# Condition weights read as four consecutive rows per partition, in a fused adaLN and feed-forward kernel on Trainium2

## The reference

```python
out = jnp.einsum('bsd,bdh->bsh', x, W[cat_ids]) + b[cat_ids][:, None, :]   # condition stage
x = act_qdq(out)
up = act_qdq(x @ lpbq_dequant(w_up).T)
gate = act_qdq(x @ lpbq_dequant(w_gate).T)
gate = act_qdq(gate * fixed_qdq_u16(jax.nn.sigmoid(gate)))
return x_in + act_qdq(gate * up) @ lpbq_dequant(w_down).T
```

## Time and profile before

| | |
|---|---|
| median of 3 runs | 970.74 us (969.74 to 971.73) |
| the profiled execution's own time | 973.98 us |
| its span, first to last instruction | 972.1 us |
| TensorE busy | 891.0 us, 92% of the span |
| VectorE busy | 656.1 us, 67% |
| ScalarE busy | 422.9 us, 43% |
| share of the chain that ended last | PE 87%, DMA 7%, ACT 3%, DVE 1% |

### The profile page before, as it was taken

How to read it: one execution, slowest core, us unless ns; L and a number is a source line. 1 busy time by engine, 2 the same in 40 slices (tenths; PEclk the granted TensorE clock), 3 DMA queues, 4 the chain that set the end, 5 groups by cost and what they waited for, 6 DMA issues and landing times.

```text
span 972.1 us, 13026 instructions
## 1 busy us (share of the span) xinstructions
PE 891.0 (92%) x4712; PEld 478.5 (49%) x4712; DVE 656.1 (67%) x771; ACT 422.9 (43%) x448; POOL 3.0 (0%) x12
## 2 busy tenths in 40 slices
PE   6999999999999999999999999970059999999998
PEld 6998995444444444444444444430024444444443
DVE  1355869655757454379899889559977777775511
ACT  1112326223223323299798872229865444444000
POOL 0000000000000000000000000000000000000000
PEclk9999999999999999999999999995569999999999
DMA  8998982544474343779999735999986799988221
GB/s 294 380 386 283 325 314 86 155 154 159 151 248 129 119 142 136 220 287 421 409 371 394 255 143 216 415 422 358 417 318 260 292 339 340 342 307 303 86 87 65
DMA packets 93875, 255.89 MB, mean 263 GB/s; under 512 B 32082, under 2 KB 32082, under 8 KB 93842
## 3 DMA queue, kind: packets, MB, share of 16 engines
q1 hardware_dynamic: 58354, 198.72, 55.3%
q10 hardware_dynamic: 35488, 56.77, 16.6%
HBM read 175.51 MB, written 73.66 MB: 256 GB/s over the span
## 4 chain that ended last, share of the span: by engine, by line
PE 87%; DMA 7%; ACT 3%; DVE 1%; issue 1%; SPq 0%; ACTq 0%; POOL 0%; DVEq 0%
PE bank L737 16%; PE bank L739 16%; PE bank L738 16%; PE bank L684 11%; PE bank L772 7%; PE bank L773 6%; PE bank L774 6%; DMA up_ring<-up_scratch 3%; DMA x_ring<-in_x_dram 2%; ACT umag L633 2%; PE bank L669 1%; PE wt_bank L772 1%; PE bias_bank L772 1%; PE wt_bank L773 1%; PE wt_bank L774 1%; PE bias_bank L773 1%
## 5 line engine op out<-in xcount | busy, mean ns | idle before, releaser
L548 ACT ACTIVATE stage<-bank 128x512 f32<-128x512 f32 x192 | 112.0, 594 | 224.6 <-PE bank L739 170.3
L772 PE MATMUL bank<-wt_down,o_even 128*128 128x512 f16 x192 | 74.0, 385 | 65.9 <-DVE o_even L1205 65.9
L996 DVE TENSOR_REDUCE tile_max<-stage 128x1 f32<-128x1536 f32 (+1 forms) x62 | 108.4, 1749 | 33.8 <-ACT stage L548 30.7
L737 PE MATMUL bank<-xq_head,wt_up 128*128 x336 | 127.4, 379 | 0.9 <-ACT stage L548 0.9
L737 PE MATMUL bank<-xq_head,wt_gate 128*128 (+1 forms) x336 | 127.4, 379 | 0.3 <-DVE xq_head L983 0.3
L738 PE MATMUL bank<-xq_head,wt_up 128*128 x336 | 127.3, 379 | 0.0
L739 PE MATMUL bank<-xq_head,wt_up 128*128 x336 | 127.3, 379 | 0.0
L739 PE MATMUL bank<-xq_head,wt_gate 128*128 (+1 forms) x336 | 127.3, 379 | 0.0
L738 PE MATMUL bank<-xq_head,wt_gate 128*128 (+1 forms) x336 | 127.3, 379 | 0.0
L684 PE MATMUL bank<-xt,w_ring 128*128 128x128 f32 x1024 | 123.4, 280 | 2.2 <-ACT xt L486 2.2
L684 PEld LDWEIGHTS bank<-xt,w_ring 128*128 128x128 f32 x1024 | 120.7, 197 | 2.5 <-issue 2.5
(11 more groups left out here) (164 smaller groups left out, 1293.8 us busy)
## 6 DMA issues: line engine op xcount, KB each, us to landing
up_ring<-up_scratch SPq DMA_DIRECT2D x60, 768.0 KB, 7.5
w_ring<-in_L_cond_W_dram SPq DMA_DIRECT2D x32, 1024.0 KB, 7.2
gate_scratch<-stage ACTq DMA_DIRECT2D x32, 768.0 KB, 3.4
gate_ring<-gate_scratch SPq DMA_DIRECT2D x32, 768.0 KB, 8.9
up_scratch<-stage ACTq DMA_DIRECT2D x32, 768.0 KB, 7.7
product_scratch<-prod_ring SPq DMA_DIRECT2D x19, 768.0 KB, 7.5
back_ring<-product_scratch SPq DMA_DIRECT2D x19, 768.0 KB, 12.8
gate_even<-gate_scratch SPq DMA_DIRECT2D x16, 768.0 KB, 7.2
```

The source lines that it names most:

```text
L548: nc.scalar.activation(stage[:, q % 2, n % PIECE_TILES, :], psum[n % BANKS][:, :], ACT.Copy)\
L737: nc.tensor.matmul(bank[:, :], w_hi, x_hi, start=(k == 0), stop=False)
L772: nc.tensor.matmul(bank, o_hi, wt_down[:, 0, k, :], start=(k == 0), stop=False)
L996: V.tensor_reduce(tile_max[:, side, bass.ds(Q * i + q, 1)], stage[:, q % 2, :, :].rearrange("p t c -> p (t c)"), AX.X, ALU.max, apply_abso ...
```

## The change

Four edits. (1) `w_ring` takes row 4p + k of W in partition p, slice k: each partition reads four consecutive rows. So that the product is the same, `turn_x` takes for slice k every fourth column of x (columns k, k+4, k+8, ...) instead of 128 neighbours. (2) At the start x of batch 1 is issued behind x of batch 0, ahead of the first W; the later x loads of the first chunk move up by one place. (3) The `w_gate` loads that stood behind W of batches 5, 7, 9, 11 stand behind W of batches 7, 8, 9, 11, and VectorE's `gate_blocks` move from behind batches 7, 9, 11, 12 to behind batches 11, 12, 13, 14; `weight_steps` moves from behind batch 13 to behind batch 14, `weight_scale` stays behind batch 15. (4) ScalarE waits for `wscale_ready` behind `copy_xt` of batch 17 instead of ahead of that of batch 16.

```diff
                 sp.dma_start(w_ring[:, r, :, :],
-                             cond_w[bass.ds(cat, 1), :, :].rearrange("a (k p) h -> p (a k) h", p=P))\
+                             cond_w[bass.ds(cat, 1), :, :].rearrange("a (p k) h -> p (a k) h", k=KH))\
...
-            load_x_batch(0, 0, True)
+            for r in range(2):
+                load_x_batch(0, r, True)
             sp.wait_ge(idx_in, 16)
             for r in range(BPC):
                 load_w_batch(0, r, True)
-                if r < BPC - 1:
-                    load_x_batch(0, r + 1, True)
+                if r < BPC - 2:
+                    load_x_batch(0, r + 2, True)
...
-                    if gate_part is not None and r % 2 == 1:
-                        at = SLICES * (gate_part + r // 2)
+                    if r in gate_parts:
+                        at = SLICES * gate_parts[r]
...
-            load_chunk(1, 0)
-            load_chunk(2, 2)
+            load_chunk(1, {3: 0})
+            load_chunk(2, {0: 1, 1: 2, 3: 3})
...
                     copy_xt(i, r, first)
+                    if weights == 1 and r == 1:
+                        act.wait_ge(wscale_ready, 1)
...
-            act.wait_ge(wscale_ready, 1)
             cond_chunk(4, False, 1)
...
+                by_part = x_ring[:, r, :].rearrange("s (p k) -> s k p", k=KH)
                 for k in range(KH):
-                    mm = nc.tensor.transpose(psum[4 + r % 2][:, k * S:(k + 1) * S],
-                                             x_ring[:, r, k * P:(k + 1) * P], ident32[:, :])
+                    mm = nc.tensor.transpose(psum[4 + r % 2][:, k * S:(k + 1) * S], by_part[:, k, :], ident32[:, :])
...
-            def after_chunk_3(r):
-                if r == 0:
-                    gate_blocks(3)
-                if r == 1:
+            def in_chunk_3(r):
+                if r < 3:
+                    gate_blocks(r + 1)
+                if r == 2:
                     dve.wait_ge(wblocks_maxed, KH)
                     weight_steps(0, WG)
...
-            cond_chunk(1, None, lambda r: gate_blocks(0) if r == 3 else None)
-            cond_chunk(2, None, lambda r: gate_blocks(r // 2 + 1) if r % 2 == 1 else None)
-            cond_chunk(3, None, after_chunk_3)
+            cond_chunk(1)
+            cond_chunk(2, None, lambda r: gate_blocks(0) if r == 3 else None)
+            cond_chunk(3, None, in_chunk_3)
```

More of the change, by code:

```diff
@@ L343, in _, with load_chunk @@
                 load_w_batch(0, r, True)
-                if r < BPC - 1:
-                    load_x_batch(0, r + 1, True)
-            def load_chunk(i, gate_part):
+                if r < BPC - 2:
+                    load_x_batch(0, r + 2, True)
+            def load_chunk(i, gate_parts):
                 for r in range(BPC):
@@ L351, in load_chunk @@
                     load_w_batch(i, r, False)
-                    if gate_part is not None and r % 2 == 1:
-                        at = SLICES * (gate_part + r // 2)
+                    if r in gate_parts:
+                        at = SLICES * gate_parts[r]
                         sp.dma_start(wf[:, at:at + SLICES, :], wg_view[:, at:at + SLICES, :]).then_inc(wgate_in, 16)
-            load_chunk(1, 0)
-            load_chunk(2, 2)
+            load_chunk(1, {3: 0})
+            load_chunk(2, {0: 1, 1: 2, 3: 3})
             with sp.Fori(3, CHUNKS) as i:
-                load_chunk(i, None)
+                load_chunk(i, {})
             sp.wait_ge(w_low, WSLICES)
```

## The result

The changed kernel takes 968.14 us (median of 7 runs, 966.54 to 969.03), the kernel before 971.07 (median of 7). The ratio is 0.9961, 95% interval 0.9949 to 0.9973: 3.8 us faster by that ratio, between 2.6 and 5.0; the two medians differ by 2.9. Forecast were 964.7 us and 6.0 us won. Direction and range hold, the size is too large. The profiled executions lie further apart than the timed runs: the span (first to last instruction, some 1.8 us shorter than the execution's own time) went from 972.1 to 966.4 us, 5.7 less.

The account below looks back on a forecast made before the run. The condition stage was taken as bound by TensorE at 4.01 us per batch; scale 4.0, start 1.6, x loads 0.4 and turn 0 sum to 6.0 us won, median 964.7 us, range 962.0 to 973.0.

Parts of the forecast that it names:

- The scale's stall: Batches 16 and 17: moving ScalarE's wait for the scale wins 4.0 us, bounds 2.5 and 4.1.
- The chain to copy 18: VectorE's work up to the first high part, then ScalarE's copy of batch 18: done 0.6 us before it is due.
- The start: Batch 0 waits for W alone and starts at 9.7 instead of 11.34: 1.6 us won, bounds 0.4 and 4.0.
- my fear that the x ahead of it would delay it: Start: 256 KB of x now go ahead of W, costing 0.68 us if none falls into the queue's empty time.
- my two bounds: Batch 0: clock rises at the same moment, 0.8 us or less won; or early enough for full speed, 4.0 won.
- Longer rows and later gate loads: x loads up to batch 12: faster W, less 0.9 us from later gate loads; 0.4 us won, bounds -0.9 and +1.1.
- my estimate: W's 8 KB rows: some 3 beats of 32 bytes per packet beside the data make 400 GB/s instead of 418.
- The 0.9 us of queue time in my sum: DMA queue at 24 to 30 us: later gate loads leave slack unfilled, 0.9 us lost before x of batch 12.
- The turn: TensorE's transposes of x by every fourth column: 0 us taken, from a possible 0 to 13.1 us lost.
- My argument from VectorE's read of PSUM: Turn: VectorE reads 128 elements 128 bytes apart in 292 ns, as side by side, so a step costs nothing.
- Rival A: Turn: stepped reads double a transpose to 218 ns, 13.1 us lost against 6.0 won, 977.8 us; chance 0.19.

Follow-up runs that it names:

- e3: Kernel before with only the x of batch 1 issued ahead of the first W; ratio 0.9996 (0.9987 to 1.0005).
- e5: Changed kernel with the w_gate loads back behind W of batches 5, 7, 9, 11, block maxima still late; 966.75 us, ratio 0.9954 of the kernel before.
- the second comparison: Changed kernel, no edit, profiled and timed a second time against the kernel before; 967.26 us, ratio 0.9954 (0.9941 to 0.9966).
- e7: Changed kernel with nine f16 matmuls on a zeroed tile ahead of the first turn; 966.07 us, ratio 0.9945 of the kernel before.
- e4: Kernel before with only the new layout (8 KB rows of W, x turned by every fourth column); ratio 1.0002 (0.9992 to 1.0011).
- e1: Kernel before, no edit, profiled and timed a second time; ratio 0.9997 (0.9987 to 1.0007).

## Why the prediction was right, and where it was too large

*The scale's stall: right in mechanism and place, its price varies.* Of the four profiles that still have it, two lose 4.0 and 4.1 us (this pair is the kernel before) and two 2.5 (second x alone, layout alone). The wait is 2.2 us in all four; what differs is whether the clock falls at its end or soon behind it. I read the 1.6 us of clock as part of the price because the one profile had it. The timed gain of this edit alone is 2.5 us (1.4 to 3.6). This is the term that was mis-sized most: 4.0 in the sum. The timed runs bear that out, since each has its mean granted clock on record. The two profiled executions that lose 4.0 have 0.963 and 0.964. Some 65 us at the lower level, in the product stage, are in every profile and take 0.033 off the mean, and a fall at batch 16 takes off 0.0018 more, so no run with it can read 0.966. Of the 61 timed runs of the kernel before that have a clock listed, 38 read 0.966 or 0.967: at least these had the cheap form, the median run of the largest set (971.11 us, 0.967) among them.

*The chain to copy 18: right.* The high part started 5.35 us behind the first instruction of `weight_scale` (82.42 - 77.07), against 5.29 forecast, and the margin was 0.77 where I had 0.6.

*The start: 1.6 forecast.* Batch 0 starts 2.0 to 2.8 us earlier, not 1.6. W of batch 0, issued at 3.21, took 5.8 us with 2 KB rows (e3) and 5.5 with 8 KB (changed), against 6.7 before. So it is in at 9.0 and 8.7, and my fear that the x ahead of it would delay it was wrong. From 3 to 10 us the DMA engines move 320 GB/s in e3 and 356 in changed, 271 before; why the queue is fuller there no run shows. But the batch runs at the lower clock level for most of its length, so part of it is given back. The prediction laid that level to the idle wait for the second x; this is not what the traces show, since a turn already takes 1.08 us at 4.87 in the kernel before, ahead of that wait, and 1.13 us at 7.67 in the changed one, without it. Over the profiles, batch 0 ends at 16.0 to 17.4 in three that issue x second with the old layout and at 13.4 to 15.0 in the seven that issue it first without added matmuls. The means differ by 2.3 us, and each group spreads over some 1.5. Neither of my two bounds (the clock rises at the same moment, or follows the start) holds alone.

*Longer rows and later gate loads: right in direction.* Forecast 0.4 us won; 1.10 to 1.4 us of late x before, 0.41 to 0.60 after, so 0.7 to 0.8. Full, the queue moves 406 to 409 GB/s, where I took 418 for W alone among loads of 387. The `w_gate` loads go in 2 KB rows as the x loads do: of the 10.2 MB that pass from 30 to 55 us in e5, 3.9 MB are 1,914 packets of 2 KB. Weighed by bytes, 418 for the other 61% gives 405. By the Trainium skill, page DMA: Bandwidth & Descriptors, section Why small descriptors are slow, my estimate had been 400 for W, which gives 395 in this mix; the trace, at 406 to 409, agrees with the row and not with that estimate. That the later gate loads cost something is shown by e5, where x is on time: 0.4 us of TensorE's time. The 0.9 us of queue time in my sum was not measured by itself.

*The turn: the step that failed.* I took 0; it costs 0.041 us per step, 4.05 against 4.01, 1.2 us over thirty. My argument from VectorE's read of PSUM did not carry over. Rival A had the sign right and the size wrong. The page Advanced Engine Details and Errata of the Trainium skill, section SBUF Cachelines, names a penalty where each access takes another line of 16 bytes, and there is one; but it is 10%, it is there at 8 bytes and smaller at 64, so lines of 16 bytes do not explain it here. Its price at a doubling, 13.1 us, was ten times too high.

With these sizes the sum is: scale 2.5 to 4.1, start 2.3, x loads 0.7, turn -1.2, so 4.3 to 5.9. Timed were 3.8 us (2.6 to 5.0) and, in the second comparison, 4.5 (3.3 to 5.7). The lower end, with the cheap form of the stall that most timed runs had, agrees with both. Two things stay open. The second x alone won only 0.4 us timed where its profile shows 1.1 at batch 0; the form of the stall does not explain it, as among the runs with a clock of 0.966 or more it is 0.5 us too. And the edits timed singly add up to 2.7 us (2.5, 0.4 and -0.2, each to within about 1), with the later gate loads never timed alone on the kernel before, while all four together won 3.8 and 4.5.

*Profile against timed runs.* The profiles of this pair differ by 5.7 us in span. The first profile of before had both a late rise of the clock (batch 0 until 17.4, 1.4 us later than in the other two with this start) and the dear form of the stall. It was the slowest execution of this kernel that I saw at 973.98, over the range of its first three runs, and I took its losses as the kernel's losses. That this pair differs by nearly the 6.0 us forecast is in part luck: term by term, up to the gate product, it shows 4.0 for the scale, 2.4 for the start (1.6 forecast), 0.7 for the x loads (0.4) and -1.2 for the turn (0), so that what I had too small and what I had left out cancel.

## What to carry to other kernels

A wait placed ahead of a queue's next instruction should stand at the instruction that needs its value: here `copy_xt` needed no scale. Ask what follows behind it in its new place and by how much it is in time, since 1.7 us more of work there brought 1.0 us of the stall back. Where the profiled execution lies above all the timed ones, its stalls may be in their dear form; take a second profile before you price the clock. And when an edit makes transfers faster, try the old schedule with it: the later gate loads gave back part of what the longer rows had won.

## What was unexpected of the hardware

- The clock can fall at an idle gap of 1.06 us (e7, f16 matmuls and short turns ahead of it) and can hold over one of 2.24 us (e3, e4, long f32 batches ahead of it), and the same 2.2 us gap has both outcomes in two profiles each. The fall need not come in the gap: in e1 TensorE had been at work again for 1.4 us, at the higher level, when it came. Work that was useless as such, 17 matmuls, saved 1.8 us together with the gate loads' old places.
- The record of the granted clock reads 1.00 in the first microseconds of the trace of before (10.0 to 17.4 too), though 23 of the 32 matmul records of batch 0 are 213 ns apart, where 112 is the pace of the higher level; there only durations tell the level.
- An f32 transpose whose weights are read with a step takes 113 to 120 ns instead of 109, for steps of 8 to 64 bytes, with no threshold at 16.
- 8 KB rows moved about as fast as 6 KB rows: 406 to 409 GB/s in a mix of which 39% of the bytes are in 2 KB rows, at 387 by themselves. By that W goes, as an estimate, at some 419 to 424, against 417 and 418 for 6 KB rows alone.
